# First group of a four-part transformer block: the order of loads, conditioning and LayerNorm before the first projection

## What is computed

```
ada = (cond @ ada_w + ada_b)[:, None, :]          # 256 -> 6 * 256
shift1, scale1, gate1, shift2, scale2, gate2 = split(ada, 6)
x1 = ln(x) * (1 + scale1) + shift1                # eps 1e-6, over the 256 features
qkv = x1 @ qkv_w + qkv_b                          # 16 heads of 128
x = x + gate1 * (softmax(q k^T / sqrt(128)) v @ out_w + out_b)
x2 = ln(x) * (1 + scale2) + shift2
x = x + gate2 * (gelu(x2 @ ffn_w1 + ffn_b1) @ ffn_w2 + ffn_b2)
```

## Time and profile before

| | |
|---|---|
| median of the runs | 1023.72 us |
| profiled execution, own time | 1027.99 us |
| its span, first to last instruction | 1026.3 us |
| PE busy | 944.8 us, 92% |
| DVE, ACT, POOL busy | 617.0, 434.0, 254.7 us |
[...]
| first projection matmul starts | 40.44 us |

### The profile page before, as it was taken

One profiled execution on the slowest core, in us unless ns is written; L12 is line 12 of the kernel. 1 busy time (PEld: TensorE's weight loads), 2 busy tenths in 40 slices (PEclk: granted clock), 3 DMA queues, 4 the chain that ended last, 5 costly groups with the idle time before them and its releaser, 6 DMA issues.

```text
span 1026.3 us, 18758 instructions
## 1 busy us (share of the span) xinstructions
PE 944.8 (92%) x7276; PEld 781.0 (76%) x7276; DVE 617.0 (60%) x1669; ACT 434.0 (42%) x1147; POOL 254.7 (25%) x340
## 2 busy tenths in 40 slices
PE   6499999999999999999788897999998559999998
PEld 4377888878877888777666565889885359999997
DVE  1555455455465545445664454467766888888887
ACT  1132322332222322223456453655542456666665
POOL 0745600020000200002022444233220264343343
PEclk9699999999999999999999998999999779999999
DMA  5122100000000000000240000000000000000000
GB/s 209 62 83 83 42 1 1 1 2 1 2 1 1 2 1 1 1 2 2 82 174 0 0 0 1 1 1 2 1 2 1 1 0 2 22 1 23 2 22 22
DMA packets 5029, 21.98 MB, mean 21 GB/s; under 512 B 592, under 2 KB 720, under 8 KB 4432
## 3 DMA queue, kind: packets, MB, share of 16 engines
q1 hardware_dynamic: 4944, 20.82, 5.6%
HBM read 18.72 MB, written 2.10 MB: 20 GB/s over the span
## 4 chain that ended last, share of the span: by engine, by line
PE 78%; issue 8%; DVE 8%; POOL 3%; ACT 2%; DMA 1%; POOLq 0%; SPq 0%; DVEq 0%; ACTq 0%
PE ps L308 36%; PE ps L591 7%; PE ps L595 6%; PE ps L508 6%; PE ps L372 5%; PE ps L590 4%; PE ps L498 3%; PE ps L510 3%; PE ps L315 2%; PE ps L361 2%; DVE frs L1249 1%; PE ps L396 1%; POOL xc L1361 1%; DVE BD L966 1%; DVE g_lo L1075 1%
## 5 line engine op out<-in xcount | busy, mean ns | idle before, releaser
L308 PE MATMUL ps<-x_hi,W_hi 128*128 128x512 f32 x256 | 109.2, 427 | 18.5 <-DVE x_lo L919 16.3
L936 DVE SCALAR_TENSOR_TENSOR o_lo<-ps,vec,o_hi 128x512 fp32r<-128x512 f32 x64 | 48.0, 750 | 110.4 <-ACT o_hi L674 110.2
L1356 POOL TENSOR_TENSOR xc<-xc,rs 128x1024 f32<-128x1024 f32 x5 | 13.2, 2644 | 366.7 <-DVE rs L915 227.1
L658 ACT ACTIVATE qk<-ps,vec 128x512 f32<-128x512 f32 x64 | 44.0, 688 | 138.4 <-PE ps L308 138.4
L308 PE MATMUL ps<-x_lo,W_hi 128*128 128x512 f32 x256 | 101.1, 395 | 0.0
L308 PE MATMUL ps<-x_hi,W_lo 128*128 128x512 f32 x256 | 101.1, 395 | 0.0
L591 PE MATMUL ps<-rk_th,cpc 128*128 128x128 f32 x512 | 98.9, 296 | 0.1
L925 DVE TENSOR_SCALAR qk<-ps,vec 128x512 f32<-128x512 f32 x64 | 47.5, 742 | 77.4 <-PE ps L308 77.4
L674 ACT ACTIVATE o_hi<-ps,vec 128x512 fp32r<-128x512 f32 x64 | 44.0, 688 | 115.8 <-PE ps L372 115.8
L508 PE MATMUL ps<-ht,hh 128*128 128x128 f32 x512 | 78.1, 285 | 2.3 <-DVE ht L1154 2.3
L591 PEld LDWEIGHTS ps<-rk_th,cpc 128*128 128x128 f32 x512 | 72.8, 192 | 8.4 <-ACT rk_th L876 5.9
(11 more groups left out here) (229 smaller groups left out, 2226.1 us busy)
## 6 DMA issues: line engine op xcount, KB each, us to landing
stage<-qkv_w SPq DMA_DIRECT2D x7, 768.0 KB, 4.2
stage<-out_w SPq DMA_DIRECT2D x4, 512.0 KB, 3.8
f_raw<-ffn_w SPq DMA_DIRECT2D x2, 1024.0 KB, 6.6
xorig<-xT SPq DMA_DIRECT2D x1, 2048.0 KB, 8.3
out<-xtb SPq DMA_DIRECT2D x4, 512.0 KB, 3.1
ada_sb<-ada_w SPq DMA_DIRECT2D x1, 1536.0 KB, 8.2
x_all<-xT SPq DMA_DIRECT2D x1, 1536.0 KB, 14.1
BD<-qkv_w SPq DMA_DIRECT2D x1, 768.0 KB, 9.5
```

The lines of the kernel that those rows point to most:

```text
L308: r = pe.matmul(out_, lhsT, rhs, start=first and i == 0, stop=last and i == n - 1)
L658: act.activation(qk[:, 0, h % 2, :], ps[:, PJ[0], :], ACT.Identity, bias=col("qkv_b", HU * u + h)).then_inc(act_evac, 1)
L936: dve.scalar_tensor_tensor(o_lo[:, h % 2, :], ps[:, OB[h % 2], :], col("qkv_b", 2 * HEADS + HU * u + h), o_hi[:, h % 2, :].bitcast(F32), A ...
```

## The change

SP's order becomes: first group of x, cnd, the first four of 12 conditioning tiles of ada_w, vec, the two weight tiles of unit 0, the other eight conditioning tiles, one weight tile of unit 1 into a new place called early (over sq and xc of group 1), the rest of x. PE runs 40 matmuls on idle before the mean, makes four conditioning tiles (shift1 and scale1) before the variance, and eight after it, the first-chunk matmuls twice as wide but for the last tile of each part; then 56 matmuls on idle. ACT loads its table for Sqrt at the start and for Exp after x_hi, makes W_hi of tile 0 ahead of the root, and x_hi by chunk. DVE makes W_lo of tile 0 ahead of the reciprocal and of tile 1 behind it, then the whole scaling and shifting of group 0 in place of GpSimd, x_lo by chunk, the bias of the other eight tiles, and clears BD. GpSimd starts with the splits when x_lo is done, the first one out of early. Group 1's center waits until early is split.

```
+ADA_FIRST = 4
+IDLE_LOAD, IDLE_FIRST = 40, 56
...
+        early, early_end = place("early", [P, 3, HU * DH], F32, x_off + 8 * KB)
...
+            sp.dma_start(x_all[:, :, 0:GT], xT[:, :, 0:GT]).then_inc(ld_x0, 16)
+            sp.dma_start(cnd[:, :, :], cond).then_inc(ld_v, 16)
+            sp.dma_start(ada_sb[:, :, 0:first], ada_w[:, :, 0:first]).then_inc(ld_ada, 16)
             sp.dma_start(vec[:, :], vecs).then_inc(ld_v, 16)
...
+            sp.dma_start(flat(stage), qkv_w[0, :, 1, :]).then_inc(ld_w[1], 16)
+            sp.dma_start(ada_sb[:, :, first:], ada_w[:, :, first:]).then_inc(ld_ada2, 16)
+            sp.dma_start(flat(early), qkv_w[1, :, 0, :]).then_inc(ld_early, 16)
             sp.dma_start(x_all[:, :, GT:TOK], xT[:, :, GT:TOK]).then_inc(ld_x, 16)
...
+            def ada_tiles(lo, hi, home):
+                for j in range(lo, hi):
+                    for c in range(KC):
+                        m = cnd[:, c, :]
+                        if c < KC - 1 and j < hi - 1:
+                            r = pe.matmul(home(j, 2 * B), ada_sb[:, c, j * P:j * P + P], m.unsqueeze(1).to_broadcast([P, 2, B]),
+                                          start=c == 0, stop=c == KC - 1)
+                        else:
+                            r = pe.matmul(home(j, B), ada_sb[:, c, j * P:j * P + P], m, start=c == 0, stop=c == KC - 1)
+                r.then_inc(ada_mm, 1)
+
+            def idle_matmuls(n):
+                for _ in range(n):
+                    pe.matmul(ps[:, PJ[0], 0:P], idle[:, :], idle[:, :], start=True, stop=True)
+
             pe.wait_ge(consts, 1)
+            idle_matmuls(IDLE_LOAD)
             ln_mean(0)
...
+            ada_tiles(0, ADA_FIRST, lambda j, n: ps[:, OB[0], j * B:j * B + n])
             ln_var(0)
+            pe.wait_ge(ld_ada2, 16)
+            ada_tiles(ADA_FIRST, 12, lambda j, n: ps[:, YB[(j - ADA_FIRST) // 4], (j - ADA_FIRST) % 4 * B:(j - ADA_FIRST) % 4 * B + n])
+            idle_matmuls(IDLE_FIRST)
...
+            act.preload_act_table(ACT.Sqrt)
             act.wait_ge(consts, 1)
             ln_square(0)
+            first_high(0, BD[:, 0:12, :])
             ln_sqrt(0)
...
+            first_high(1, stage)
+            for c in range(KC):
+                act.wait_ge(mod0, 4 + c)
+                act.activation(x_hi[0][:, c, :], xc[0][:, c, :], ACT.Copy).then_inc(hi0, 1)
+            act.preload_act_table(ACT.Exp)
...
             def ln_center(g):
                 dve.wait_ge(ln_pe, 2 * g + 1)
+                if g == 1:
+                    dve.wait_ge(pool_w, 2)
...
+            ada_add(0, ADA_FIRST, lambda j: ps[:, OB[0], j * B:j * B + B])
+            first_low(0, BD[:, 0:12, :])
             ln_recip(0)
...
+            first_low(1, stage)
+            dve.wait_ge(ln_dve, 2)
+            dve.tensor_tensor(xc[0][:, :, :], xc[0][:, :, :], rs[:, :].unsqueeze(1).to_broadcast([P, KC, GT]),
+                              ALU.mult).then_inc(mod0, 1)
+            dve.wait_ge(ada_dn, 1)
+            by_b = xc[0][:, :, :].rearrange("p c (b t) -> p c b t", t=T)
+            for i, (which, op) in enumerate(((SCALE1, ALU.mult), (SHIFT1, ALU.add))):
+                for c in range(KC):
+                    dve.wait_ge(mod0, i + 1 + i * c)
+                    dve.tensor_tensor(by_b[:, c], by_b[:, c], ada_rows(which, 0, c), op).then_inc(mod0, 1)
+            for c in range(KC):
+                dve.wait_ge(hi0, c + 1)
+                r = dve.tensor_tensor(x_lo[0][:, c, :], xc[0][:, c, :], x_hi[0][:, c, :].bitcast(F32), ALU.subtract)
+            r.then_inc(x1_lo, 1)
+            dve.wait_ge(ada_mm, 2)
+            ada_add(ADA_FIRST, 12, lambda j: ps[:, YB[(j - ADA_FIRST) // 4], (j - ADA_FIRST) % 4 * B:(j - ADA_FIRST) % 4 * B + B])
             dve.wait_ge(w_rdy, 1)
             dve.memset(BD[:, :, :], 0.0).then_inc(ada_dn, 1)
-            low(0)
...
             pool.wait_ge(ada_dn, 1)
-            modulate(xc[0], rs, SCALE1, SHIFT1, 0, ln_dve, ln_pool)
+            pool.wait_ge(x1_lo, 1)
...
-                pool.wait_ge(ld_stage, 16 * (n + 1))
+                pool.wait_ge(*((ld_stage, 16 * n) if n else (ld_early, 16)))
```

More of the change, by code:

```diff
@@ L256, in _, with flat @@
         def _(sp):
+            def flat(tile):
+                return tile[:, :, :].rearrange("p a b -> p (a b)")
+            first = ADA_FIRST * P
+            sp.dma_start(x_all[:, :, 0:GT], xT[:, :, 0:GT]).then_inc(ld_x0, 16)
+            sp.dma_start(cnd[:, :, :], cond).then_inc(ld_v, 16)
+            sp.dma_start(ada_sb[:, :, 0:first], ada_w[:, :, 0:first]).then_inc(ld_ada, 16)
             sp.dma_start(vec[:, :], vecs).then_inc(ld_v, 16)
-            sp.dma_start(cnd[:, :, :], cond).then_inc(ld_v, 16)
-            sp.dma_start(x_all[:, :, 0:GT], xT[:, :, 0:GT]).then_inc(ld_x0, 16)
-            sp.dma_start(ada_sb[:, :, :], ada_w).then_inc(ld_ada, 16)
             sp.dma_start(BD[:, 0:12, :].rearrange("p a b -> p (a b)"), qkv_w[0, :, 0, :]).then_inc(ld_w[0], 16)
-            sp.dma_start(stage[:, :, :].rearrange("p a b -> p (a b)"), qkv_w[0, :, 1, :]).then_inc(ld_w[1], 16)
+            sp.dma_start(flat(stage), qkv_w[0, :, 1, :]).then_inc(ld_w[1], 16)
+            sp.dma_start(ada_sb[:, :, first:], ada_w[:, :, first:]).then_inc(ld_ada2, 16)
+            sp.dma_start(flat(early), qkv_w[1, :, 0, :]).then_inc(ld_early, 16)
             sp.dma_start(x_all[:, :, GT:TOK], xT[:, :, GT:TOK]).then_inc(ld_x, 16)
-            n = 0
+            n = 1
             for u in range(1, NU + 1):
-                for kc in range(KC if u < NU else 0):
-                    if n == 0:
+                for kc in range(u == 1, KC if u < NU else 0):
+                    if n == 1:
                         sp.wait_ge(w_rdy, 2)
@@ L643, in ln_sqrt @@
                 act.wait_ge(ln_pe, 2 * g + 2)
[L644 to L645 removed]
+                if g == 1:
+                    act.wait_ge(x1_lo, 1)
+                if g > 1:
+                    act.wait_ge(ln_pool, 3 * (g - 1))
                 act.activation(rs[:, :], ps[:, TB, :], ACT.Sqrt, bias=eps_t[:, 0:1]).then_inc(ln_act, 1)
             def high(g):
[L649 removed]
+                act.wait_ge(ln_pool, 3 * g)
                 act.activation(x_hi[g % 2][:, :, :], xc[g % 2][:, :, :], ACT.Copy).then_inc(x1_hi, 1)
@@ L675, in out_high, with first_high @@
                                bias=col("qkv_b", 2 * HEADS + HU * u + h)).then_inc(ohi_done, 1)
+            def first_high(kc, src):
+                act.wait_ge(ld_w[kc], 16)
+                act.activation(W_hi[:, 0, kc, :, :].rearrange("p a b -> p (a b)"), src[:, :, :].rearrange("p a b -> p (a b)"),
+                               ACT.Copy).then_inc(w_hi0, 1)
+            act.preload_act_table(ACT.Sqrt)
             act.wait_ge(consts, 1)
             ln_square(0)
+            first_high(0, BD[:, 0:12, :])
             ln_sqrt(0)
[L681 to L685, removed]
+            first_high(1, stage)
[3 more added lines that the diff above has]
+            act.preload_act_table(ACT.Exp)
             for h in range(HU):
@@ L997, in gate, with ada_add, first_low @@
                     dve.tensor_tensor(group(x_all, g, c), group(x_all, g, c), scratch, ALU.add).then_inc(gate_done, 1)
+            def ada_add(lo, hi, home):
+                for j in range(lo, hi):
+                    one = 1.0 if j // 2 in (SCALE1, SCALE2) else 0.0
+                    r = dve.tensor_scalar(ada[:, j, :], home(j), col("ada_b", j), one, ALU.add, ALU.add)
+                r.then_inc(ada_dn, 1)
+            def first_low(kc, src):
+                dve.wait_ge(w_hi0, kc + 1)
+                dve.tensor_tensor(W_lo[:, 0, kc, :, :].rearrange("p a b -> p (a b)"), src[:, :, :].rearrange("p a b -> p (a b)"),
+                                  W_hi[:, 0, kc, :, :].rearrange("p a b -> p (a b)").bitcast(F32),
+                                  ALU.subtract).then_inc(w_rdy, 1)
             ln_center(0)
@@ L1002, in _ @@
             dve.wait_ge(ada_mm, 1)
[L1003 to L1007, removed]
-            ln_recip(0)
[L1010 to L1015, removed]
+            ada_add(0, ADA_FIRST, lambda j: ps[:, OB[0], j * B:j * B + B])
+            first_low(0, BD[:, 0:12, :])
+            ln_recip(0)
+            first_low(1, stage)
[14 more added lines that the diff above has]
+            ada_add(ADA_FIRST, 12, lambda j: ps[:, YB[(j - ADA_FIRST) // 4], (j - ADA_FIRST) % 4 * B:(j - ADA_FIRST) % 4 * B + B])
             dve.wait_ge(w_rdy, 1)
             dve.memset(BD[:, :, :], 0.0).then_inc(ada_dn, 1)
-            low(0)
             for h in range(HU):
@@ L1024, in _ @@
             value(0, 3)
-            dve.wait_ge(ada_dn, 2)
+            dve.wait_ge(ada_dn, 3)
             soft_c(0)
@@ L1351, in _, with modulate @@
             TT, TS = pool.tensor_tensor, pool.tensor_scalar
-            def modulate(buf, factors, which_scale, which_shift, g, s_dve, s_pool):
-                pool.wait_ge(s_dve, 2 * g + 2)
```

(6 more changed lines are left out.)

14 lines of the change are left out of this document (8 added, 6 removed).

## The result

The changed kernel takes 1012.32 us in the median of four executions (1010.46 to 1013.47), the kernel before beside it 1024.26 (1023.22 to 1027.89); the ratio is 0.9872, 95% interval 0.9838 to 0.9906. Twelve microseconds are gained. The forecast was 1007.0 with a range from 1004.3 to 1011.0, so the direction is right, and the time lies above the range.

The account below looks back on a forecast made before the run. The prediction took a serial line to the first projection at 40.44 us, then a full PE, as the bound; 16.3 (earlier start) + 0.4 (clock) - 0.2 = 16.5 off the 1023.7 median gave 1007.2, said as 1007, range 1004.3 to 1011.

Parts of the forecast that it names:

- the first one: Start of the kernel before: one serial line to the first projection at 40.44 us, 12 conditioning tiles taking 10.43 of it.
- the same 16.5 us: Whole kernel: the summed saving, 16.3 + 0.4 - 0.2, taken off the median of 1023.7.
- first projection 40.4 to 24.1: 16.3: Start of the kernel: the first projection comes at 24.1 in place of 40.4 us, gaining 16.3.
- The rival of a slow PE (B): Start: PE stays at half clock and bounds it, first projection about 29.5, gain 11, total 1012.7; B's band 23%.
- a fall before the second tiles: Conditioning: clock falls only before its second part, start at 27 with a warm start, 1008.5; within B's 23%.
- Idle matmuls ahead of the mean: During the wait for x: 40 raise PE's clock, cost about 0.1 us; the mean takes 2.4, to 8.6.
- Conditioning in two parts: Around the variance: four tiles take 1.8 us, eight take 3.6 hidden behind DVE; conditioning leaves the chain.
- DVE's line: Ahead of the first projection: DVE's splits, reciprocal and moved LayerNorm set the start at 24.1 us, bounds 23.3 to 25.
- tables: Start, ACT: the preload hides a 1.28 us table load under the wait for x; otherwise the start slips by 1.28.
- Idle matmuls behind the conditioning: Before the first projection: 56 take 3.1 us, PE then idles 3.7; clock falls anyway, gain 0 to 1.87, taken 0.4.
- Added work ahead of the first keys: Behind the first projection: DVE is free 3.4 us after it; first key done at 2.7, PE needs it evacuated at 4.1.
- GpSimd's tiles: Behind the first projection: two weight tiles split 10 to 11 us after it, wanted 20.5 after; later tiles keep that lead.

Follow-up runs that it names:

- b2: The kernel before, unchanged, profiled once more: 1022.91 us.
- a2: The changed kernel, unchanged, in a further profiled execution: 1010.34 us.
- a1: The changed kernel, unchanged, in a further profiled execution: 1008.2 us.
- e3_noidle: Both runs of idle matmuls left out of the changed kernel (0 and 0 in place of 40 and 56): 1015.29 us, ratio 0.9908 to the kernel before.
- e5: Changed kernel with scaling and shifting (LayerNorm) of the first group put back on GpSimd: 1013.64 us, ratio 0.991 to the kernel before.
- e6: Changed kernel with all 12 conditioning tiles ahead of the variance and the second ada_w piece loaded ahead of the weight tiles: 1014.96 us, ratio 0.9926.
- r_after: The changed kernel again, unchanged, beside the kernel before in five rounds: 1010.78 us, ratio 0.9862.
- e1_hold: Changed kernel with 100 idle matmuls in place of 56 behind the conditioning: 1012.71 us, ratio 0.9885 to the kernel before.
- e4: The kernel before with only 40 idle matmuls added ahead of the mean: 1025.26 us over 12 executions, ratio 1.0019.
- b1: The kernel before, unchanged, profiled once more: 1027.74 us.
- i1: The kernel before with only 40 idle matmuls added ahead of the mean, profiled again: 1027.53 us.
- e2_hold160: Changed kernel with 160 idle matmuls in place of 56 behind the conditioning: 1014.88 us, ratio 0.991 to the kernel before.
- i2: The kernel before with only 40 idle matmuls added ahead of the mean, another profile: 1027.12 us.

## Why the prediction missed its range

**The step that failed is the first one**: the start at 40.44 and the conditioning at 10.43 us were taken as properties of the kernel, and the difference was taken off the median. Of the five profiles of this kernel two have this start, three one of 34.7 to 35.0, and most unprofiled executions have the times of the latter. The profiled execution's own time, 1027.99, stood 4.3 us above the median. The prediction wrote this down and drew nothing from it; it should have asked which stretch of the trace was 4 us long by chance. Taken off the 1027.99 of the execution from which its rows came, the same 16.5 us give 1011.5, beside the measured 1012.3: the saving was sized well for an execution like that one, and put on the wrong base. The term "first projection 40.4 to 24.1: 16.3" measured 16.2 (24.27) to 17.1 (23.30) against a like execution, and 10.4 to 11.7 against the usual one (34.7 to 35.0 less 24.3 to 23.3). Together with what the first 24 matmuls gain where the clock holds (7.51 in b2, 5.88 in a2) this accounts for the 12 of the medians: b2 to a2, 12.6 us, are 11.4 at the start and 1.6 in these matmuls, and the rest goes the other way.

The forecast gain was 16.7 us (1023.72 to 1007), the measured one 11.9 (1024.26 to 1012.32): 4.8 too much, and the other 0.5 of the miss is the median of the kernel before, which moved. A start at 40.44 in place of 34.7 to 35.0 is 5.4 to 5.7 us, and 4.6 to 4.9 of them are the conditioning. Nor is PE slow up to the start in the trace that the rows come from: the variance of the earlier trace rows, 21.24 to 24.17, takes 2.93 us, between the 3.75 of the mean and the 1.94 of the variance in b2, so the clock rose within it.

The rival of a slow PE (B), the one with a time near the measured 1012, is not what happened: in none of the four profiles did PE bound the start. Its milder form, a fall before the second tiles, did occur in a1 and a2; but the clock came back at 18.2 and 19.3, and PE was done at 23.0 and 23.2, not at 27. That the measured time lies near B's is luck.

**Idle matmuls ahead of the mean.** 40 in 3.75 to 4.45 us from 1.68 and the mean in 1.79 to 2.53: right. What they buy at the start is less than it seemed: e3_noidle lost 1.1 us there in its one profile, though both runs of idle matmuls together are worth 4.5 in the medians.

**Conditioning in two parts, DVE's line, tables.** Right within 0.4 us each, and the start with them; only the second piece of ada_w landed 0.6 to 0.9 us later than forecast, off the chain. e5 prices the move of the LayerNorm at about 3 us, e6 the split at 3 to 4. One reading behind DVE's line was wrong: the W_lo of 1.70 us is not a row "where GpSimd is quiet", since GpSimd's product runs beside it, from 28.42 to 32.08. That product takes 3.66 us there and 2.40 in the later groups (at 120.78), and the next W_lo 3.89; the lengths come out as if the two engines took turns (29.80 to 32.08 waited, then 1.61), which is an estimate from these rows. With GpSimd quiet, in the changed kernel, both splits took 1.6 to 1.8.

**Idle matmuls behind the conditioning.** The expected fall came in the shown profile and in r_after: pauses of 2.49 and 3.00 us, in the first a granted clock of 0.77 in 23 to 24 us, in the second of 0.78 in 24 to 25, then 0.50 in both, and 7.24 and 7.32 us for the 24 matmuls. a1 and a2 went the other way, by a slow conditioning whose idle matmuls ran into the pause and left 0.31 us of it. How long PE is slow at the start varies from one execution to the next: among the five of the kernel before the conditioning alone differs by 4.9 us (5.56 to 10.43).

**Added work ahead of the first keys.** With the clock held the first 24 matmuls take 5.88 where the later 24 take 5.48 in the earlier trace rows: 0.4 us late. No run shows the 0.2 that the sum takes off for this; it was the author's estimate. In e1_hold, where the start came 2.0 us after x_lo, they take 5.54. With the clock down DVE was done first: it waited 0.92 us for PE ahead of the first key in the changed kernel as shown, and 1.02 in r_after.

**GpSimd's tiles.** PE is busy 342.70 of 343 us behind 27: no wait came in their place. The first two tiles were split at 33.97, 10.2 us behind the first projection, as worked out.

**The range** held the bounds of the changed kernel's costs and none for the kernel before. A lower bound of the old conditioning, 48 instructions at the 0.11 of the earlier trace rows (5.3 us), stood among the rows of the prediction; with it the range would have reached about 1012.

## What to carry to other kernels

Before rows are added up, compare the profiled execution's own time with the median. Where the two are apart, take the difference off the time of the execution that the rows come from, or find the stretch that could have gone otherwise, and bound it by the rows of the same instruction at the other clock. Work at the start of this kernel, which is bound by PE, had two prices from one execution to the next (10.43 us or 5.56 to 5.79 for the conditioning): a forecast needs both, for the kernel before as for the kernel after. Taking PE's narrow matmuls off the chain took the gamble out of the start: it lies at 23.3 to 24.3 in four profiles, with the clock lost or held behind the variance. Idle matmuls alone (e4) did not: five of 12 executions were long with them, one of 17 without.

## What the runs showed of the hardware

- 48 conditioning instructions of 64 columns take 10.43 or 5.56 to 5.79 us in the same kernel, 0.22 or 0.12 each; in b1 (10.43) and b2 (5.79) with the same mean of 3.75 us ahead of them.
- PE busy without a gap did not bring the clock back: in i1 it fell at 12.6 us, 1.7 us after a wait of 1.8 us had ended, and stayed at 0.50 for 9 us in which PE was busy 9.00 of 9.00 us with 64-wide matmuls. In a1 it came back at 18.2 within the instructions of the second part, which are 64 and 128 wide.
- The wait for the second piece of ada_w is the longer, the earlier the mean ends: 2.54 us with a mean ended at 7.5 (a1), 1.77 at 8.1 (as shown), 1.27 at 8.6 (r_after), 0.40 at 9.2 (e3_noidle). Where it was 2.18 to 2.54 us (e2_hold160, a2, e1_hold, a1) the clock fell 0.3 to 1.8 us after it had ended; where it was 0.40 to 1.77 (e3_noidle, r_after, as shown) it held through the second part. In the kernel before with idle matmuls, waits of 1.80 and 1.86 (i1, i2) ahead of 64-wide matmuls lost it.
- The column of granted clock reads 1.00 from 10 to 20 us in b1, where the 48 conditioning instructions take 10.43 us against 5.79 in b2, and from 7 to 11 in the trace of before, where the four matmuls of the mean take 3.75 us against 1.72 at 61.14. So in these traces the column does not tell the level ahead of its first change (at 26.5 in b1, 26.8 in before), and the durations do.
- Where GpSimd's product and DVE's W_lo met, the one that started first kept its length and the other was lengthened: W_lo took 1.70 us from 28.19 and the product, from 28.42, 3.66 in place of 2.40; the next W_lo, begun beside it, took 3.89, against 1.61 and 1.76 in the changed kernel. In e5 the same pair shows 1.69 and 3.75.
